# Masks added by VectorE: the attention maxima and the windowed exponentials of a five-layer kernel

## The chip, the cores and the metric
The kernel runs on one core of a Trainium2 chip. The metric is the device time of one execution in microseconds; the time before is the median of three runs.

## The reference
16 sequences of 256 tokens and 256 features go through five attention layers of 16 heads (16 features each), with float32 inputs and outputs: `self` and `cross` (each with an integer mask over query and key, then layer norm, then, behind `cross`, a feed-forward part), `l1` (no mask), `l2` (one key and value head for all, and a window: a query sees the keys from 64 before to 64 after it) and `l3` (no mask, then a second feed-forward part). What the change touches is the masked softmax:

```python
energy = jnp.where(mask == 0, jnp.float32(-1e+20), energy)          # self, cross
attn = jax.nn.softmax(energy / jnp.sqrt(jnp.float32(E)), axis=-1)
...
keep = _window_mask(S)                                              # l2
scores = jnp.where(keep[None, None], scores, NEG)
probs = jax.nn.softmax(scores, axis=-1)
attn = jnp.matmul(probs, v)
```

## The kernel before
A sequence is worked as a list of steps, and each layer's attention goes through its heads twice. In the steps `max0` to `max7` (two heads each, a *unit*) TensorE computes the scores with queries on the partitions into a bank of PSUM (`scores_for_max`, L1290 the mask, L1294 the scores) and VectorE takes minus the maximum over the keys (L1144) into `neg_max`. GpSimd cuts four units' maxima into three bfloat16 pieces (`pieces0`, `pieces1`, L844 to L850), TensorE turns them (`turn0`, `turn1`, L1434), ScalarE copies them out (L934), and a DMA puts them under the queries as three more rows. In the steps `exp0` to `exp7` TensorE computes the scores again, now with keys on the partitions and with the maximum subtracted by those rows (`scores_for_exp`; masks L1314 and L1318, scores L1321 and L1326), and ScalarE takes the exponential into one of four buffers of `probs` (L927). `weigh0` to `weigh3` multiply them with the values (L1347 to L1358); each waits for the exponentials of its two units. Every unit has two halves, t or k = 0 and 1, each in one bank of 2 x 256 float32; for `l2` only the 192 keys or queries in reach are computed, so a bank holds 2 x 192.

The masks are bfloat16 tiles of 0 and -2^66: `neg_self` and `neg_cross`, made by GpSimd (L785), and the constant `neg_band` for `l2`. A mask reaches a bank in one of two ways. Either TensorE multiplies it by an identity with start=True and lets the scores accumulate on it, or the unit is *primed*: ScalarE copies the mask into the bank ahead of the scores (steps `pre0` and so on for maxima, `prx0` and so on for exponentials, L912) and TensorE adds the scores to it. `PRIMED` has for each masked step and each of the 16 sequences eight bits, one for each unit, that say which are primed.

The order of all steps of all sequences is one list, `SCHEDULE`, written out as the string `ORDER`: each character names a lane (0 to f are the sequences' main chains, A to P the work beside them, s the setup, Q to l the priming steps), and takes the next step of that lane. Three or so sequences are in work at a time. Every engine and the DMA queue walk the same list in order and do their own part of each step, with semaphores between them; `place_banks` deals the eight PSUM banks out by the same list.

Of the kernel before, what the change touches and what calls it, by code (L numbers as in the profile page):

```python
# [8 lines left out]
ALU = mybir.AluOpType  # L9
# [14 lines left out]
MASKED = -float(2 ** 66)  # L24
LAYERS = ["self", "cross", "l1", "l2", "l3"]
# [42 lines left out]
for _name in BIAS_SOURCES:  # L68
# [15 lines left out]

PRIMED = {
    ("self", "max"): (
        "00010000 00010010 00001110 01100111 00000001 00000111 00010111 00001111 "
        "01111111 00000001 00000000 00000000 00000000 00010111 01001011 00000100"),
    ("cross", "max"): (
        "11100000 10011111 00000000 11011110 01000100 10000000 11011111 00110001 "  # L90
        "00101000 11110111 00111110 00011100 11100000 00000000 10110101 01001001"),
    ("l2", "max"): (
        "00110000 01000001 10001110 10111111 00110000 10111101 00101101 01101101 "
        "00101000 01000000 00000010 11001100 00011101 10001100 01001100 00000110"),
    ("l2", "exp"): (
        "00000000 10000000 00000000 00000000 00000000 10010000 00000000 00000000 "
        "10100000 00000000 10100000 00000000 10010000 00000000 10100000 00100100"),
# [43 lines left out]
def beside_steps():  # L141
# [8 lines left out]
    "AQ0sA0ss0S0A0Q0AA000QA0BA00001ABsAs0B0A00QA0Q0sAA00R0B101Q0110Q1110BsA11000s00BsRBA01R11R0R1A0RA1001"  # L150
    "0021B1101011AA0CR0s11s1C0020222BBs10001B1121QCQ0Q100BB0s01B1s0CQ0C00001120Q12202100S101S0022012s22SB"
    "02CB0S010Q01QD2BQS2010ss0012S211B10A200RB22R0011s210122AR22R210R1012R20R101211CR01200AAs122sA111102C"
    "0CC0100C12C011111212011001112C0C011110121C00210021010CC20102C20001010002002102B101C2B2000210B202211B"
    "CB201222121022S212122S21221C2121E1122221C1Q02Q120111C200110120S0C11S1221121SQ1010Q120011S002R20012s1"
    "0012R11Q101220100RR200212S00R100120002R10201RQ102R00A21201S11102RR121A0Q1QA20112011112B12A0101E20212"
    "22A10112202022B020221Q2222120Q00R12000012022100200D210200022220122000B1SS0B00B1S02S22S02S0212D01SS20"
    "0222211021201220D02222122S212111102D21Q2021021101D2032S13311231333112301T33232DT13132113T3TC2TC1D2U1"
    "CU331T3T1CC3131331D222333S321333D21333D3E11DDE222U13322D1E3321221331E22432D402F4U2344424EUD144224DDD"
    "2F244242E1234EVE2432QE4UF2224U34E44E2433443V444E2344TE42FE43422443T42ET4T344F23T3423T4323F4RU3E344T4"
    "UTFE2UF3G4SF24F3FF345423U5443F3344U533343U44334345435353335444345343543355VV5553VD5D34534534V45U54V3"  # L160
    "4D4434F44435F5345DUD433555554534433555F35354435552343533F544335343F3G545533335435F45V534333335E45354"
    "5V453355V54E4E5E35353555V443E5F3544555344454555V54544545544534545344454334455TT433544F534F3334TT4435"
    "V4T435UF4T53433TV5454T3433V53U44343T353F5544D3435TUU3344344D5D3453D434D43533544U4W444E4E44354U4555E5"
    "44344554EH44U5554G534445UE545U353454453444545545435355G534435455344543533444435345434344344354444333"
    "534343434V433U433345533335V43X33V443334T55WU3354553VV45VV33534453V54V7VG3355335666GH55V65646655G566W"
    "XG6G5555555556H65G55FGG66W7X77W56G65776675HW6H7W6F67675F35676677565X66FH676657HF5HHHHG677X6H5X7X67G7"
    "7656T6H77557577H6775757575H5H4757775777755IH5765756753755U6756H757XX65HG57V5X56777GX7X7XGG755755755H"
    "5X6777766567775W6777W75576IW56HW5I6566HW5IW6H57H76X685WW8776766I7776688668877668Y66667866768Y7667786"
    "788Y7786Y8767886YI6677668877766YY67I688778777686876878857G86887G8878687867G7J7G7668G7678I8I676788777"
    "678I6766767III7I686I686786776I6J87III68Y866Y886H7Y766678Y6668868878Y666788X8668787867878H688878X886X"  # L170
    "87X87788Y88X8777886YHXH77678I686X8668W7H877Z8I778888Y6IWWI68W6W78777777877X867786W77IWK66877W6668688"
    "76X678876687Z66666W68688W6J86667J6688786786887866788777788G86G788G68X8867G78786G77876876878687677776"
    "866X7766768677766767766786Y787Y87686877Y8676667Y6667688866YY66786766Y78W68Y7h6Y6868878Z68KYg8766a668"
    "99Z989gg897988988899898Z8888JI8Z8gJWI9X98I9898gIYh98I98Jh68J88JK9J9Z8989JhJ89898998g9Jaaaa99K9J8g896"
    "98a89889hh9888a99aJ88K9a999aJ888888L9aa8Kaaa898J8978a89aJ8K8La89aZh98J8K9a98K99aaZ8aaaK89aZKKaZaL89a"
    "K989a89Ka8L9Z9Z8L89bbbaaZ8bbZL9bb9aaaK8aKJbb9b9a99Ka99bbabLba99aKK999gabbJ99b999b99bJLg9bab9Jb999Jba"
    "9gabaaa9L99L9baagaa9gb9Lbbgababb9bga9baga9bbbLabY9abb9b9a99abLLa9aaLbLaaa9LaL9Mbaaa99a9aa9ba9abhL999"
    "bL9ba9ahb9baMh9L99a9ab99aL9bhbhbba9ah9abZbabbLbaab9L9a9bKaa9bbb9aKbKaabbKbbbbb9Kabiabb9bb9aba9aabb9a"
    "ba9999Zb9Zbaabbab99baaagag9bha9hba9a9aba9aZaaibZ9baaa999ab99aab9aZb9bgaZ99b999g9ba9JbbgbK9babb999abb"
    "99iMabZ9bJbJba9baa9b9bbaZagJbbaNagi9bab9bb9aaZbJNag9baiK9abaabbbK9Kg9LgaKb9a9abL9aab9a99Laaab9a99aLa"  # L180
    "a999aabhbbbabL9a99a9bh9bhZhahbbbagh9ahibbab999M99999bbb999baabab9b9abbbba9baabab999ibbbaabbMb9aja9aa"
    "hb9a99cabachcbhacacacMcbMNabcMccMa9bacaMacbaaccbaaaac9MccabcababaccMcbaaccMbcbaccMbbabbcccbNbabccbca"
    "cbaccccbMcbcMbacbbiMbcaNNiacaccZMaONcMcbaciicccdcbcbNbcbiacNbbcNbcNbbbccicicbicbNcdddcOcddbOcdNjccbc"
    "MccbdcbcbccddcdbObcjcbbdecdecejeedOeeceebcejdceMcdcejddcjdNMgkkcdhddedcdkedkcMecdOddcckddMddeeNkddcd"
    "OddeceddckecdecceNddcNOeeecdecNeecNeeccPdecOOOeeccdOOcbcedceddecedecOcPcceceOdddcddcOccedcdOcdeddccc"
    "ddedcdecdOdehejeOecdkddddddeckidecedkekkeeddedckcekikMdecceecejddejdjdMeecccjedeMdciiidMddcieMceceic"
    "ddecceeiedjidcNdeNccicjeNeidcNcjecedcdcPNcecceccdddccecdecceddcdedcddcceePeedcddcccdedecdedecOccOcdd"
    "dddcedOdelccdcedcceddcOcdOededccdcceeccdcececdeecccccecedeececcedceedlccdededciekeeeccjejedcdjeejeed"
    "eceejcecddePjcdcPedkflddffeddejkffecddeeedddeddedPdlkdddefddfffkldeedfdkkeeNNNNedejedekkdkfefdeeePef"
    "leeedjfeNffdededeeffPfdeedfdflPPPffPPdeffdfPeffPfffdkfddfdffdfPfdeffdPPdcefdjdffdeddfededfddflfddOle"  # L190
    "edflfdlfdeddfefffOddlldlfefflfffeefOPffOfdOffPefeffdfffefeffefffefdeeffPjfPfedefefdffdfdefeffeeeefdd"
    "PdffdfffdffffkefeefeeffdeeffffeefefefllPffPffPffffelllffefffefPfefefefPeffeelfefffllfffffffefffefllf"
    "ffffflelffffffffffffffjffffffffffffffffffffffffffffffffffffffffffffffffff"
# [75 lines left out]
FIRST_MASKED = {}  # L269
for _key in SCHEDULE:  # L270
    if _key[2][:3] == "max" and primer(_key) is None:
        FIRST_MASKED.setdefault(_key[:2], _key)
PRIME_NO = Numbers(lambda l, step: step[:3] in ("pre", "prx"))
MAX_NO = Numbers(lambda l, step: step[:3] == "max")
EXP_NO = Numbers(lambda l, step: step[:3] == "exp")
WEIGH_NO = Numbers(lambda l, step: step.startswith("weigh"))
# [92 lines left out]
def width(l):  # L369
    return BAND if l == "l2" else S  # L370


def build(nc, x, ctx, x_features, ctx_features, mask_cross, mask_self, params, setup_params, out):
    stack = ExitStack()
    with stack:
# [98 lines left out]
        exped = sem("exped")  # L474
        weighed = sem("weighed")
# [503 lines left out]
        def _(dve):  # L979
# [148 lines left out]
            def run(keys):  # L1128
                for key in keys:
# [5 lines left out]
                    elif step[:3] == "max":  # L1135
                        u = int(step[3:])
                        n = HALF_NO.place[b, l, f"max{u // 4 * 4}"]
                        if u % 4 == 0 and n >= HALVES:

                            last = HALF_NO.earlier(key, HALVES)  # L1140
                            dve.wait_ge(max_cut, PIECES_NO.upto(last[:2] + (f"pieces{int(last[2][3:]) // 4}",)))
                        for t in range(T):
                            bank = wait_full_unit(dve, key, t)
                            v.tensor_reduce(neg_max[:, n % HALVES, t, 2 * (u % 4):2 * (u % 4) + 2], bank[:, :, 0:width(l)],  # L1144
                                            AX.X, ALU.max, negate=True).then_inc(maxed, 1)
                    elif step in ("ksplit", "qsplit"):
# [504 lines left out]
```

## Time and profile before

| | |
|---|---|
| median of 3 runs | 2375.08 us (2370.65 to 2376.75) |
| profiled execution | 2372.76 us |
| its span, first to last instruction | 2370.6 us |
| granted TensorE clock, mean | 0.984 |
| TensorE matmul busy | 2256.6 us, 95% |
| VectorE busy | 1599.6 us, 67% |
| ScalarE busy | 1297.4 us, 55% |
| GpSimd busy | 517.9 us, 22% |

Busy time is the union of an engine's instructions; instructions of one engine overlap at their ends, so that the time from one start to the next is shorter than the time of one. A row names the line of the kernel, the engine, the operation, what it writes and reads, and how often it ran.

### The profile page before, as it was taken

What the parts mean: (1) busy time and instruction counts of PE and PEld (TensorE: products, weight loads), DVE (VectorE), ACT (ScalarE), POOL (GpSimd) and SP (SyncE); (2) the same over time, 40 slices, a digit from 0 to 9 for tenths busy, and PEclk for the clock granted to TensorE, in tenths of its full rate; (3) what the DMA queues carried; (4) which work ended last, traced back from release to release, by engine and by line L of the source; (5) the groups of instructions that cost most, each with busy time, mean ns of one, the idle gap of its engine ahead of it and who ended that gap; (6) DMA issues with size and microseconds to landing.
All of it is one profiled execution on the core that took longest, in us unless ns stands there. A gap on an engine that the chain in (4) does not pass through costs nothing.

```text
span 2370.6 us, 50134 instructions
## 1 busy us (share of the span) xinstructions
PE 2256.6 (95%) x18291; PEld 1715.8 (72%) x18291; DVE 1599.6 (67%) x3311; ACT 1297.4 (55%) x2723; POOL 517.9 (22%) x1120
## 2 busy tenths in 40 slices
PE   6999999999998999999999999999999999999966
PEld 4777777777776776877767677877778677777744
DVE  6767687775767677576675767676856767586432
ACT  3554556665464656656464656456465654654522
POOL 4221112231112232121212312111232211122100
PEclk9999999999999999999999999999999999999987
DMA  7322213321212133222122332122231321122100
GB/s 224 114 74 60 60 51 86 105 72 35 77 42 69 33 97 82 63 56 71 40 55 71 100 81 58 48 56 72 67 87 51 83 64 42 51 61 53 48 12 12
DMA packets 164242, 159.17 MB, mean 67 GB/s; under 512 B 17824, under 2 KB 162720, under 8 KB 162976
## 3 DMA queue, kind: packets, MB, share of 16 engines
q1 hardware_dynamic: 164000, 155.97, 24.0%
q8 instruction: 148, 2.42, 0.4%
q14 instruction: 94, 0.77, 0.1%
HBM read 35.71 MB, written 4.19 MB: 17 GB/s over the span
## 4 chain that ended last, share of the span: by engine, by line
PE 68%; issue 18%; DVE 5%; POOL 4%; POOLq 3%; ACT 2%; DVEq 1%; DMA 1%; SPq 0%; ACTq 0%
PE bank L1265 16%; PE bank L1255 12%; PE bank L1294 8%; PE bank L1347 7%; PE bank L1326 6%; PE bank L1290 3%; PE bank L1318 3%; PE bank L1246 3%; PE bank L1466 2%; DVE neg_max L1144 2%; PE bank L1321 1%; PE bank L1314 1%; POOL resid L781 1%; POOL rstd L771 1%; PE bank L1496 1%
## 5 line engine op out<-in xcount | busy, mean ns | idle before, releaser
L1144 DVE TENSOR_REDUCE neg_max<-bank 128x2 f32<-128x512 f32 (+1 forms) x1280 | 762.5, 655 | 217.6 <-PE bank L1294 210.7
L927 ACT ACTIVATE probs<-bank 128x512 f32<-128x512 f32 (+1 forms) x1280 | 645.9, 585 | 325.2 <-PE bank L1326 273.4
L1265 PE MATMUL bank<-par,hidden_t 128*128 128x256 f32 x1792 | 418.9, 384 | 6.3 <-ACT hidden_t L862 3.4
L1265 PEld LDWEIGHTS bank<-par,hidden_t 128*128 128x128 f32 x1792 | 334.1, 191 | 58.8 <-ACT hidden_t L862 9.3
L1326 PE MATMUL bank<-query_stack,key_stack 99*128 99x256 bf16 x2048 | 344.4, 274 | 7.2 <-DMA query_stack<-max_rows 4.0
L1294 PE MATMUL bank<-key_stack,query_stack 96*128 96x256 bf16 x2048 | 326.8, 276 | 16.2 <-issue 13.7
L1255 PE MATMUL bank<-tok_t,par 128*128 128x256 f32 x1408 | 334.6, 387 | 4.4 <-ACT tok_t L862 4.4
L1255 PEld LDWEIGHTS bank<-tok_t,par 128*128 128x128 f32 x1408 | 262.2, 193 | 42.6 <-ACT tok_t L862 7.1
L1294 PEld LDWEIGHTS bank<-key_stack,query_stack 96*128 96x128 bf16 x2048 | 195.9, 99 | 111.1 <-issue 33.4
L1347 PE MATMUL bank<-probs,values 128*17 128x256 f32 x4096 | 256.9, 382 | 1.8 <-DVE neg_max L1144 0.9
L1326 PEld LDWEIGHTS bank<-query_stack,key_stack 99*128 99x128 bf16 x2048 | 194.1, 98 | 62.1 <-issue 12.7
L844 POOL CAST max_pieces<-neg_max 128x16 bf16<-128x16 f32 x160 | 37.2, 232 | 821.8 <-DVE neg_max L1144 797.1
L1347 PEld LDWEIGHTS bank<-probs,values 128*17 128x17 f32 x4096 | 102.0, 97 | 109.4 <-issue 29.5
L961 ACT ACTIVATE hidden_t<-bank,par 128x256 f32<-128x256 f32 x256 | 107.0, 472 | 115.5 <-PE bank L1255 114.8
L1029 DVE TENSOR_TENSOR summed<-bank,resid 128x512 f32<-128x512 f32 x64 | 44.1, 690 | 121.3 <-PE bank L1265 121.3
L769 POOL TENSOR_SCALAR var_eps<-mv 128x2 f32<-128x2 f32 x112 | 25.6, 229 | 426.6 <-DVE mv L1000 423.8
L1164 DVE TENSOR_TENSOR hidden_t<-bank,recip 128x256 f32<-128x256 f32 x160 | 99.7, 623 | 12.3 <-issue 0.4
L934 ACT CAST max_rows<-bank 24x256 bf16<-24x256 f32 x160 | 57.0, 356 | 92.1 <-PE bank L1434 91.9
L1318 PE MATMUL bank<-ident_b,neg_self 128*128 128x256 bf16 x512 | 98.3, 273 | 0.0
L1318 PE MATMUL bank<-ident_b,neg_cross 128*128 128x256 bf16 x512 | 97.9, 272 | 0.1
L862 ACT COPY tok_t<-bank 128x512 f32<-128x512 f32 x96 | 56.5, 589 | 72.1 <-PE bank L1246 71.4
L771 POOL TENSOR_TENSOR rstd<-var_eps,minus_half 128x2 f32<-128x2 f32 x128 | 91.6, 716 | 19.4 <-issue 0.9
(167 smaller groups left out, 3271.9 us busy)
## 6 DMA issues: line engine op xcount, KB each, us to landing
query_stack<-query_pieces SPq DMA_DIRECT2D x480, 128.0 KB, 2.4
key_stack<-key_pieces SPq DMA_DIRECT2D x384, 128.0 KB, 2.4
c_in<-in_ctx SPq DMA_DIRECT2D x16, 256.0 KB, 3.3
tok_t<-in_x_features SPq DMA_DIRECT2D x16, 256.0 KB, 2.8
m_in<-in_mask_self SPq DMA_DIRECT2D x16, 256.0 KB, 3.1
x_in<-in_x SPq DMA_DIRECT2D x16, 256.0 KB, 3.1
ctx_t<-in_ctx_features SPq DMA_DIRECT2D x16, 256.0 KB, 3.1
m_in<-in_mask_cross SPq DMA_DIRECT2D x16, 256.0 KB, 3.4
```

Source lines behind the costliest of these rows:

```text
L771: g.tensor_tensor(rstd[:, n % MOMENTS], var_eps[:, n % ROOTS], minus_half[:], ALU.pow).then_inc(rstd_ready, 1)
L927: a_.activation(probs[:, n % PROB_BUFS, k, :, 0:width(l)], bank[:, :, 0:width(l)], ACT.Exp, scale=SCALE[l]).then_inc(exped, 1)
L961: last = a_.activation(hidden_buffer(b, l)[:, f, :], bank[:, k, :], func, bias=pv(bias)[:, f:f + 1])
L1144: v.tensor_reduce(neg_max[:, n % HALVES, t, 2 * (u % 4):2 * (u % 4) + 2], bank[:, :, 0:width(l)], AX.X, ALU.max, negate=True).then_inc(max ...
L1164: v.tensor_tensor(out_tok(b, l)[:, t, :].rearrange("p (c d h) -> p h c d", c=C, h=HC), slots[:, :, 0:HD].rearrange("p (h c) d -> p h c d", ...
L1246: last = pe.transpose(bank[:, c, t * P:(t + 1) * P], src[:, t, c * P:(c + 1) * P], ident[:])
L1255: last = pe.matmul(bank[:, k, :], pv(weight, C)[:, c, column + k * P:column + (k + 1) * P], src[:, c, :], start=(k == 0 and c == 0), stop= ...
L1265: last = pe.matmul(bank[:, t, :], src[:, t * P:(t + 1) * P], weight, start=(t == 0 and n == 0), stop=(n == len(parts) - 1), skip_group_che ...
L1294: last = pe.matmul(bank[:, i, 0:n], queries[0:ROWS, h, t * P:(t + 1) * P], keys[0:ROWS, 0 if l == "l2" else h, columns(l, t)], start=l not ...
L1318: pe.matmul(bank[:, :, t * P:(t + 1) * P], masked[:, t, k * P:(k + 1) * P], twice(ident_b[:], P), start=(t == 0), stop=False, skip_group_c ...
L1326: last = pe.matmul(bank[:, i, 0:n], keys[0:MAX_ROWS, h, k * P:(k + 1) * P], queries[0:MAX_ROWS, h, columns(l, k)], start=l not in neg and ...
L1347: last = pe.matmul(dst, values[b % SLOTS][:, k, head_in(NJ * g + j), :], p, start=(k == 0 and g % 2 == 0), stop=(k == T - 1), skip_group_c ...
```

## The change
Two more ways for the mask, chosen unit by unit by two new tables. A unit whose bit is set in `PRIMED` stays primed.

- A unit with its bit in `ADDED` (maxima of `self`, `cross` and `l2`): TensorE computes the bare scores, and VectorE does, for each of the two heads of a bank, one `tensor_tensor_reduce` that adds the mask in place, multiplies by -1 and takes the minimum, instead of one `tensor_reduce` for both heads.
- A unit with its bit in `CAPPED` (exponentials of `l2`): TensorE computes the scores with the maximum subtracted and without mask, ScalarE takes the exponential, and VectorE takes the elementwise minimum with (mask + 2^66), which is 0 out of reach and 2^66 within it. The weighing waits for VectorE's semaphore `caps` for such units.

`PRIMED` and `ORDER` are other ones, and the lane of priming steps has a `self.pre0` more and `l2.prx0 l2.prx1` in place of `l2.prx0 l2.prx2 l2.prx3 l2.prx5`. The 41 lines of `ORDER` are left out here.

```diff
+LARGEST = 3.0e38
...
+ADDED = {
+    ("self", "max"): (
+        "00000000 00000000 01100000 00111000 11000000 11111011 10000000 00001000 "
+        "11111001 00100000 10100000 10110000 00001001 11100100 01100000 00100100"),
+    ("cross", "max"): (
+        "00000000 01010111 00000010 01101010 00001000 00000000 01011011 00000000 "
+        "00000000 01110111 10100000 01111001 00000011 00101000 00000010 00000000"),
+    ("l2", "max"): (
+        "11001111 00000000 00000000 10010010 00000001 01101101 00001000 10000010 "
+        "00101010 01100010 00000000 10110000 11011000 01111010 10010000 00000111"),
+}
+CAPPED = (
+    "00000101 00000000 10000001 10000001 10100000 00100000 10100000 10100000 "
+    "01111001 11100001 10100000 00100000 00111001 11100000 00000000 10101001"
+)
 PRIMED = {
     ("self", "max"): (
-        "00010000 00010010 00001110 01100111 00000001 00000111 00010111 00001111 "
-        "01111111 00000001 00000000 00000000 00000000 00010111 01001011 00000100"),
+        "11100010 00001001 00000111 00000001 00000100 00000100 00001110 00010111 "
+        "00000110 00000100 00000000 00000000 00000000 00010011 00011100 00000010"),
     ("cross", "max"): (
-        "11100000 10011111 00000000 11011110 01000100 10000000 11011111 00110001 "
-        "00101000 11110111 00111110 00011100 11100000 00000000 10110101 01001001"),
+        "11111000 10101000 00000000 10010100 11110000 11000000 10100100 10000101 "
+        "11001100 10001000 01010110 00000000 01111000 00000000 11111101 00011110"),
     ("l2", "max"): (
-        "00110000 01000001 10001110 10111111 00110000 10111101 00101101 01101101 "
-        "00101000 01000000 00000010 11001100 00011101 10001100 01001100 00000110"),
+        "00100000 01001001 01011110 01101101 11100000 00010010 01110000 00110100 "
+        "10010001 10000000 00000000 00000100 00100101 00000101 01100000 01011000"),
     ("l2", "exp"): (
-        "00000000 10000000 00000000 00000000 00000000 10010000 00000000 00000000 "
-        "10100000 00000000 10100000 00000000 10010000 00000000 10100000 00100100"),
+        "00000000 00000000 00000000 00000000 00000000 11000000 00000000 00000000 "
+        "10000000 00000000 00000000 10000000 10000000 00000000 00000000 00000000"),
 }
...
+def added(key):
+    b, l, step = key
+    row = ADDED.get((l, step[:3]))
+    return row is not None and row.split()[b][int(step[3:])] == "1" and not primes(b, l, step)
+
+def capped(key):
+    b, l, step = key
+    return l == "l2" and step[:3] == "exp" and CAPPED.split()[b][int(step[3:])] == "1" and not primes(b, l, step)
...
+                        if key == FIRST_ADDED.get((b, l)):
+                            if l != "l2":
+                                dve.wait_ge(negs, NEG_NO.upto((b, "self", "inputs" if l == "self" else "negc")))
+                            elif b < SLOTS:
+                                dve.wait_ge(band_ready, 1)
                         for t in range(T):
                             bank = wait_full_unit(dve, key, t)
+                            if added(key):
+                                k = width(l)
+                                for i in range(2):
+                                    h = 2 * (u % 4) + i
+                                    last = v.tensor_tensor_reduce(bank[:, i, 0:k], bank[:, i, 0:k],
+                                                                  neg[l][s][:, t, 0:k], -1.0, LARGEST, ALU.add,
+                                                                  ALU.min, neg_max[:, n % HALVES, t, h:h + 1])
+                                last.then_inc(maxed, 1)
+                                continue
...
+                    elif step[:3] == "exp":
+                        if capped(key):
+                            p = probs[:, EXP_NO.place[key] % PROB_BUFS]
...
+                            for k in range(T):
+                                dve.wait_ge(exped, T * EXP_NO.place[key] + k + 1)
+                                v.scalar_tensor_tensor(out=p[:, k, :, 0:n], in0=twice(neg["l2"][s][:, k, 0:n], n),
+                                                       scalar=-MASKED, in1=p[:, k, :, 0:n], op0=ALU.add,
+                                                       op1=ALU.min).then_inc(caps, 1)
...
-                masked = neg[l][b % SLOTS] if l in neg and primer(key) is None else None
+                fresh = l not in neg or added(key)
+                masked = neg[l][b % SLOTS] if not fresh and primer(key) is None else None
...
-                                         start=l not in neg and i == 0, stop=i == 1, skip_group_check=True)
+                                         start=fresh and i == 0, stop=i == 1, skip_group_check=True)
...
-                masked = neg[l][b % SLOTS] if l in neg and primer(key) is None else None
+                fresh = l not in neg or capped(key)
+                masked = neg[l][b % SLOTS] if not fresh and primer(key) is None else None
...
-                    pe.wait_ge(exped, max(T * EXP_NO.place[b, l, f"exp{2 * g + i}"] + k + 1 for i in range(2)))
+                    exps = [(b, l, f"exp{2 * g + i}") for i in range(2)]
+                    for places, ready in ((EXP_NO.place, exped), (CAP_NO.place, caps)):
+                        left = [T * places[x] + k + 1 for x in exps if (ready is caps) == capped(x)]
+                        if left:
+                            pe.wait_ge(ready, max(left))
```

## Rows read from the trace of the kernel before
**Rows 1.** The page: the span, and each engine's busy us, share and instructions.
```profile
span 2370.6 us, 50134 instructions
PE 2256.6 (95%) x18291; PEld 1715.8 (72%) x18291; DVE 1599.6 (67%) x3311; ACT 1297.4 (55%) x2723; POOL 517.9 (22%) x1120
```
**Rows 2.** Windows: stretch and length, busy PE, PEld, DVE, ACT, POOL, clock, DMA, GB/s.
```profile
0.00:60.00 60.00, 41.42 (x279) 24.39 (x280) 41.64 (x79) 22.28 (x36) 27.90 (x43) 1.00 0.72 222
60.00:2100.00 2040.00, 1990.84 (x16397) 1524.54 (x16395) 1425.40 (x2960) 1162.14 (x2453) 453.14 (x990) 0.99 0.25 67
2100.00:2300.00 200.00, 178.61 (x1389) 135.29 (x1386) 115.51 (x240) 96.12 (x200) 32.27 (x75) 0.97 0.15 42
2300.00:2371.00 71.00, 45.67 (x232) 31.55 (x232) 17.07 (x34) 16.91 (x34) 4.57 (x13) 0.73 0.06 16
```
**Rows 3.** Windows of the tile neg_band alone: busy PE, PEld, ACT, POOL.
```profile
2100.00:2300.00 200.00, 7.88 (x24) 2.32 (x24) 3.57 (x8) 0.00 (x0) 0.97 0.15 42
```
**Rows 4.** Waits of PE: who waited for whom, us in total, times, longest.
```profile
PE bank L1246 <- DVE norm L1008: 11.8, 5, 3.7
PE bank L1434 <- POOL max_pieces L850: 9.1, 10, 2.5
```
**Rows 5.** Lines by form, PE: count, busy us, mean ns, idle before.
```profile
L1314 PE MATMUL bank<-neg_band,ident_b 128*128 128x384 bf16 x230 | 75.1, 327 | 0.4 <-DMA query_stack<-max_rows 0.2 <-ACT probs L927 0.2
L1290 PE MATMUL bank<-neg_self,ident_b 128*128 128x512 bf16 x176 | 68.3, 388 | 11.3 <-issue 11.1 <-DVE neg_max L1144 0.2
```
**Rows 6.** Timeline of PE: start, us, instruction, count; cross masks and scores.
```profile
1081.12 0.38 PE L1290 MATMUL bank<-neg_cross,ident_b 128*128 128x512 bf16 x1
1081.34 0.38 PE L1294 MATMUL bank<-key_stack,query_stack 96*128 96x256 bf16 x2
```
**Rows 7.** Timeline of PE: local masks, with a local score behind each.
```profile
1142.71 0.33 PE L1314 MATMUL bank<-neg_band,ident_b 128*128 128x384 bf16 x1
...
1144.03 0.33 PE L1314 MATMUL bank<-neg_band,ident_b 128*128 128x384 bf16 x1
```
**Rows 8.** Lines by form, ACT: the priming copies.
```profile
L912 ACT CAST bank<-neg_cross 128x512 f32<-128x512 bf16 x112 | 62.1, 600 | 3.2 <-DVE neg_max L1144 3.0
L912 ACT CAST bank<-neg_band 128x384 f32<-128x384 bf16 x130 | 58.4, 495 | 5.6 <-DVE neg_max L1144 4.9 <-DVE key_rest L1058 0.5
```
**Rows 9.** Timeline of DVE: tensor_tensor_reduce on SBUF, with its accumulator read.
```profile
317.82 0.43 DVE L1216 CUSTOM_DVE_ANT_0 hidden_t<-norm 128x256 f32<-128x256 f32 x1
318.17 0.08 DVE L1216 DVE_READ_ACCUMULATOR2_ANT sumsq<- 128x1 f32 x1
318.17 0.42 DVE L1216 CUSTOM_DVE_ANT_0 hidden_t<-norm 128x256 f32<-128x256 f32 x1
```
**Rows 10.** Timeline of DVE, and its group by form: the wide maxima.
```profile
1080.08 4.88 DVE L1144 TENSOR_REDUCE neg_max<-bank 128x2 f32<-128x512 f32 x8 [3.53 <-PE bank L1294]
L1144 DVE TENSOR_REDUCE neg_max<-bank 128x2 f32<-128x512 f32 x1024 | 636.9, 682 | 155.6 <-PE bank L1294 151.0 <-POOL max_pieces L850 1.4
```
**Rows 11.** Timeline of DVE: local maxima, and one alone.
```profile
1148.15 1.48 DVE L1144 TENSOR_REDUCE neg_max<-bank 128x2 f32<-128x384 f32 x3
L1144 DVE TENSOR_REDUCE neg_max<-bank 128x2 f32<-128x384 f32 x256 | 125.6, 549 | 61.9 <-PE bank L1294 59.7 <-POOL max_pieces L850 1.3
```
**Rows 12.** Lines by form, DVE: two-input operations by width and source.
```profile
L1029 DVE TENSOR_TENSOR summed<-bank,resid 128x512 f32<-128x512 f32 x64 | 44.1, 690 | 121.3 <-PE bank L1265 121.3
L1024 DVE SCALAR_TENSOR_TENSOR resid<-hidden_t,rstd,par 128x256 f32<-128x256 f32 x96 | 42.5, 483 | 5.7 <-POOL rstd L771 5.6
L1208 DVE SCALAR_TENSOR_TENSOR hidden_t<-hidden_t 128x512 f32<-128x512 f32 x16 | 11.0, 687 | 5.0 <-ACT hidden_t L966 4.8
```
**Rows 13.** The page's groups: GpSimd's cast of maxima.
```profile
L844 POOL CAST max_pieces<-neg_max 128x16 bf16<-128x16 f32 x160 | 37.2, 232 | 821.8 <-DVE neg_max L1144 797.1
```
**Rows 14.** Timelines of POOL and DVE at 1069 us.
```profile
1069.17 0.58 POOL L844 CAST max_pieces<-neg_max 128x16 bf16<-128x16 f32 x1 [3.22 <-DVE neg_max L1144]
1069.02 0.68 DVE L1041 TENSOR_TENSOR key_rest<-ctx_t,key_pieces 128x512 f32<-128x512 f32 x1
```

More of the change, by code:

```diff
@@ L129 @@
 PRIMES = (
-    "self.pre2 self.pre1 self.pre3 self.pre4 self.pre6 self.pre5 self.pre7 cross.pre0 cross.pre2 cross.pre1 "
-    "cross.pre3 cross.pre4 cross.pre5 cross.pre7 cross.pre6 l2.pre0 l2.pre1 l2.pre2 l2.pre3 l2.pre4 l2.pre5 "
-    "l2.pre7 l2.pre6 l2.prx0 l2.prx2 l2.prx3 l2.prx5 "
+    "self.pre0 self.pre2 self.pre1 self.pre3 self.pre4 self.pre6 self.pre5 self.pre7 cross.pre0 cross.pre2 "
+    "cross.pre1 cross.pre3 cross.pre4 cross.pre5 cross.pre7 cross.pre6 l2.pre0 l2.pre1 l2.pre2 l2.pre3 l2.pre4 "
+    "l2.pre5 l2.pre7 l2.pre6 l2.prx0 l2.prx1 "
 )
@@ L155 @@
[L155 to L164, printed above, removed]
@@ L190 @@
[L190 to L193, printed above, removed]
+    "s00sAAARsAA00000Q00QQS0QAAAAsB01AA0QA0BBQ0As0BQ0A0000101100Q101R0B1B01BA0001R0s0A00ss011AR11001A0S0R"
@@ new lines @@
+    "sRCR10C1B1R10110s1121A00221s20112B00s10Cs01BB111SQQ00BSsQ0Q01S001Q110Q20s01B0002B120C0220100B1C0B012"
+    "0BQB2C200112200B01SQs020102S21S0211s202A20100R2212212AA2R2010RTR2s1R1R1A000RA1C011DR2102011020021C12"
+    "11C101C102C012112C11Cs0C211010011s1001211102012001210C100C02122C20C21C01211000B002000120210210B1202B"
+    "BB01200C2210221T2S0212S1221S012SC22122Q1S2C111R21122211221Q1000S201011C12S111S0221Q02011100021102120"
+    "1C201211Q0Q0211022QRR010000021RRQ0R2102E1010022000Q010RERT121012AV21011A01220s1201111A20B11122101012"
@@ new lines @@
+    "0A2121R10A2122202102B2TR020212202222001000221202120B002S001T20020200000SS2210121B02T2002D2S0SS21Q202"
+    "021002S2S1022B12120Q220202222VS12221D0111222100D2121011112T01323331D233DU33332112D011311331223111E1U"
+    "CT3231C1CCD3C123U1U133322223313331D233033312D312232132D31D2S23V31D1D33213224ED3422434E244243D4421224"
+    "F22DEE42D24U344E4DEE2EU224U444F34T43F22E4T422343E4U1E42ET4F4E24424433E4234F4T44EF3234T4323T2334344T3"
+    "33324TF243F4EU544F42U4F3344UF3U3434F53334344535343V3354554434353355D34VV35553335U534VD53U45V55U34444"
@@ L194 @@
+    "flffOfdlOflelddfflfeffeffdfkefdOffffffeefffffOfdfeeeffffkfedPeefedfffPfeeedfdfefePfdfddfdfPfffdeffee"
+    "ffefeefeffeffefeefeffefefPfffffffdeeffflfeffefefefefflfPefefPfleflfPfflefflfflfffefffeffffPffffflfff"
+    "fffffffffffflffffflffffffffffffffffffffffffffffffffffffff"
 )
@@ L268 @@
 WORK_NO = Numbers(lambda l, step: step in THROUGH_WORK)
-FIRST_MASKED = {}
+FIRST_MASKED, FIRST_ADDED = {}, {}
 for _key in SCHEDULE:
     if _key[2][:3] == "max" and primer(_key) is None:
-        FIRST_MASKED.setdefault(_key[:2], _key)
+        (FIRST_ADDED if added(_key) else FIRST_MASKED).setdefault(_key[:2], _key)
 PRIME_NO = Numbers(lambda l, step: step[:3] in ("pre", "prx"))
@@ L275 @@
 EXP_NO = Numbers(lambda l, step: step[:3] == "exp")
+CAP_NO = Numbers(lambda l, step: step[:3] == "exp", lambda key: capped(key))
 WEIGH_NO = Numbers(lambda l, step: step.startswith("weigh"))
@@ L474, in build @@
         exped = sem("exped")
+        caps = sem("caps")
         weighed = sem("weighed")
@@ L1322, in scores_for_exp @@
                                          queries[0:MAX_ROWS, 2 * u:2 * u + 2, columns(l, k)],
-                                         start=False, stop=True, skip_group_check=True)
+                                         start=fresh, stop=True, skip_group_check=True)
                     for i in range(2 if l != "l2" else 0):
```

63 lines of the change are left out of this document (33 added, 30 removed).

## The prediction
> **What bounds the kernel now.** I read the page's busy shares first. TensorE works 2256.6 us of a span of 2370.6 us, 95%, VectorE 67% and ScalarE 55% [rows 1]. Then the windows, which say where the missing 5% lies [rows 2]: between 60 and 2100 us TensorE is busy 1990.8 of 2040 us, so only 49 us are open there, while the start (18.6 open of 60), the last stretch of two sequences (21.4 of 200) and the end (25 of 71) hold the other 65. The reader is to see that for 86% of the time TensorE is the bound with hardly a hole, VectorE has 30% of that stretch free (1425 of 2040) and ScalarE 43%. What TensorE gives up in that stretch therefore comes off the end time nearly one for one, and what VectorE takes on costs only where it makes TensorE wait. Such waits are small today: the longest sort is 11.8 us over all, that on GpSimd's cut maxima 9.1 us [rows 4].
>
> **Count of the change.** A unit is two heads of one attention step, done in two halves of one PSUM bank each. A unit's mask reaches the bank in one of these ways: by a TensorE matmul (masked), by a ScalarE copy ahead of the scores (primed), and now also by VectorE (added, capped). Counting the 0/1 rows of the diff, with a primed bit taking precedence, gives: self maxima 88 masked and 40 primed become 61, 29 and 38 added; cross 72 and 56 become 46, 48 and 34; local (l2) 76 and 52 become 47, 40 and 41; local exponentials 115 and 13 become 87, 5 and 36 capped. The counts before agree with the trace, two matmuls a unit: 176 for self maxima, 230 for local exponentials [rows 5], and likewise 144 and 152.
>
> **TensorE, removed.** 27 + 26 = 53 self and cross units lose two mask matmuls of 512 columns, 29 + 28 = 57 local units two of 384. The mean of one (388, 327 ns) includes the tail that runs under the next; what it costs the queue is the distance to the next start. For 512 columns that is 1081.34 - 1081.12 = 0.22 us [rows 6]. For 384 columns, from 1142.71 to 1144.03 run four pairs of mask and score matmul of equal width, 1.32 / 8 = 0.165 us [rows 7]. Sum: 106 x 0.22 + 114 x 0.165 = 23.3 + 18.8 = 42.1 us. No other matmul is added or taken away. The score matmuls now open the bank themselves, which is a flag and costs nothing (bounds: that of a first-in-bank matmul like the mask's, after which [rows 6] shows no gap, so 0). Few masks lie where TensorE has holes: of 382 local ones 24 come after 2100 us [rows 3], and beside them the first units of the first sequence. I take 2 us off: 40.
>
> **ScalarE, removed.** Primed units fall by 11 + 8 wide and 12 + 8 narrow, two copies each: 38 x 0.60 + 40 x 0.495 = 42.6 us [rows 8]. ScalarE is on the critical path only in small pieces, so I book nothing; it makes room beside the exponentials, and banks are held shorter, since a primed bank is taken before its scores and an added one is not.
>
> **VectorE, added in the maxima.** An added half is two instructions that add the mask, take the minimum of the negated sum and hand over an accumulator, in place of one reduction. The trace shows this instruction only on SBUF, 256 wide: starts at 317.82 and 318.17, and the accumulator read falls in between, so 0.35 us each [rows 9]. The reduction it replaces: eight 512-wide ones in 4.88 us, the last 0.68 long, so (4.88 - 0.68) / 7 = 0.60 us [rows 10]; three 384-wide ones in 1.48, so (1.48 - 0.55) / 2 = 0.465 [rows 11]. Their difference, 0.135 us for 128 elements, puts the 192-wide new instruction at 0.35 - 0.067 = 0.283. Per wide unit 4 x 0.35 - 2 x 0.60 = +0.20 us, x 72 = 14.4; per local unit 4 x 0.283 - 2 x 0.465 = +0.20, x 41 = 8.3. Sum 22.7 us. Bounds: low 0, if from PSUM it starts no later than a reduction of the same number of elements; high, if nothing overlaps, 4 x (0.43 + 0.08) - 1.20 = +0.84 a unit, 95 us. I take 22.7, for PSUM is no slower where the trace has both: 512 elements with one operand from PSUM 690 ns, 512 from SBUF alone 687 ns [rows 12].
> The Trainium skill ("VectorE: DVE Perf Modes", the errata section) gives a PSUM source a fixed part of 120 cycles against 58; by that 452 instructions would cost 62 cycles or 0.065 us more each, an estimate of 29 us more of VectorE. By that rule the sum for VectorE would be 52 instead of 23 us; [rows 12] don't show the difference.
>
> **VectorE, added in the exponentials.** 36 units x 2 instructions of 384 elements with both tensors in SBUF. 256 elements take 483 ns and 512 take 687 [rows 12], so about 585 ns; as a reduction's last 0.08 us lie under the next (0.68 against 0.60), I take 0.505. 72 x 0.505 = 36 us; bounds 0.40 (the reduction's 0.135 us for 128 elements and nothing fixed) and 0.69 each, 29 to 50 us. Each capping waits for the exponential of ScalarE, and queued behind it on VectorE are the next maxima, whose pieces go to GpSimd, then to TensorE and to the next exponentials; the weighing of a capped unit waits for VectorE instead of ScalarE. Where the order leaves one exponential's length between, the wait is hidden. It has four buffers of probabilities for that, and each is now held about 0.5 us longer.
> VectorE in all: +59 us, so about 1659 us of 2335, 71% against 67%. In the dense stretch it goes from 70% to about 74%. That is not a bound. What is late next is a chance coincidence: a maximum that waits behind a capping. I price it at 4 us of TensorE: the two sorts of wait in [rows 4] sum to 21 us, and busy over free time of VectorE in the dense stretch rises from 0.70 / 0.30 to 0.74 / 0.26, a fifth. Bounds: -15 (a new order removes a third of the 49 open us) and +25 (the open share of the dense stretch grows by half).
>
> **GpSimd.** Its work is the same. The capping has two SBUF inputs; beside such an instruction (1069.02, two SBUF inputs) a piece cast took 0.58 us where the mean is 232 ns [rows 13, 14]. 36 cappings meet few of the 160 chains of pieces; I book nothing, bounds 0 to 3 us.
> The Trainium skill ("SBUF — State Buffer", Who interferes with whom) says that such an instruction shares its second read path with GpSimd and the one that starts later is blocked whole; the trace agrees, and the 452 new mask additions, with one SBUF input, would by it not count.
>
> **Moved.** The whole order is another one, on all queues, SP's loads and copies and GpSimd's steps too. The work and the DMAs are the same in number. After the last step of the last but one sequence comes the same chain, 65 steps and now 68, so I leave the end at its time; at the start a primed first unit makes ScalarE wait for the mask where TensorE did. Bounds for the start: 5 us either way of 18.6 open.
>
> **Sum.** 2370.6 - 40 + 4 = 2334.6 us of span; the profiled run is 2372.8, 2.1 more than its span, and the median of the runs 2375.1, 4.4 more than the span. On the median: 2375.1 - 36 = 2339 us.
>
> **Rivals.**
> 1. The new order also closes holes: the removed copies on ScalarE and shorter-held banks let TensorE run denser. For it: 49 open us in the dense stretch and 65 elsewhere. Against: the order before was as dense, and VectorE has more to do. A third to a half of the 49: 2339 - 4 - 15 to -24, about 2316 us. Chance 0.18.
> 2. The gain is mostly eaten: each 0.5 us capping and its wait stands in VectorE's queue ahead of maxima on the way to the next exponentials. If half of VectorE's added 59 us come back as waits of TensorE, 2375 - 40 + 30 = 2365 us. For it: VectorE is the next busiest. Against: 30% of it is free in the dense stretch. Chance 0.10.
> 3. Slower: the mask addition on PSUM doesn't overlap and reads both operands at half rate, so one takes about 0.69 us (the 512-element price) + 0.08, 4 x 0.77 - 1.20 = +1.9 us a unit, 113 units = 212 us, with the capping 248. VectorE then has 1848 us, 78% of the span, and in places with several added units in a row it sets the pace. It decides from the point where waits take over 40 us; at a quarter, 62 us, the result is 2375 - 40 + 62 = 2397 us. For it: the trace has no such instruction on PSUM. Against: 0.35 us on SBUF, and [rows 12]. Chance 0.06.
> 4. The change does as told, at the forecast's size: 0.66.
>
> **Range and chances.** The forecast with its own bounds (-15 to +25, VectorE's prices inside these) is 2320 to 2360. It must reach towards rival 1 and 2: 2314 to 2364 us. A change under 0.3%, 7 us, is about what can't be told from none. Faster 0.86: forecast, rival 1 and the better part of rival 2 (2365 lies 10 us below). Same 0.06, slower 0.08.
>
> **What would show it.** Mask matmuls of TensorE at 122, 92, 94 and 174, and TensorE's busy time down by 38 to 45 us; no more than 55 us open between 60 us and 270 us before the end. The new instruction pair 0.33 to 0.42 us apart from start to start; above 0.6 the third rival holds. VectorE's busy time up by 50 to 85 us, ScalarE's down by 40. Waits of TensorE on the capped probabilities below 10 us in all. The forecast is wrong if TensorE's busy time falls as said and the span doesn't.

## The result, and the profile after

The changed kernel takes 2338.16 us (median of four runs, 2336.47 to 2344.41) against 2375.41 us; the ratio is 0.9852, 95% interval 0.9829 to 0.9874, so 37 us or 1.5% faster. Measured again with six executions it was 0.9875 (0.9851 to 0.9899), 30 us. The forecast was 2339 us, with 2314 to 2364 as its range. The profiled execution was the slowest of the four, 2344.4 us; its numbers are set against the profiled one of before, 2372.8, and not against the medians. One of the four executions of run 2 below had a granted clock of 0.84 where the others had 0.98 and took 2602.9 us; the figures of run 2 are those of the other three.

The page of the changed kernel, busy us, share and instructions of each engine, for [rows 1]:
```profile
span 2342.3 us, 50407 instructions
PE 2227.5 (95%) x18071; PEld 1699.2 (73%) x18071; DVE 1675.2 (72%) x4061; ACT 1267.8 (54%) x2647; POOL 523.5 (22%) x1120
```
TensorE has 220 matmuls less, as counted. Its window rows, for [rows 2] (the last two stretches are as far from the end as there):
```profile
0.00:60.00 60.00, 43.36 (x252) 25.09 (x253) 38.54 (x74) 23.87 (x39) 27.49 (x41) 0.91 0.76 221
60.00:2072.00 2012.00, 1960.82 (x16180) 1508.88 (x16179) 1496.74 (x3677) 1128.94 (x2373) 457.99 (x991) 0.99 0.25 68
2072.00:2272.00 200.00, 177.27 (x1409) 134.25 (x1407) 122.57 (x275) 97.95 (x203) 32.98 (x76) 0.97 0.15 41
2272.00:2343.00 71.00, 46.01 (x232) 30.95 (x232) 17.36 (x37) 17.00 (x34) 5.00 (x14) 0.74 0.06 16
```
The dense stretch, from 60 us to 271 us before the end, became 28 us shorter (2012 against 2040), and the time in it in which TensorE was open (not busy) stayed: 2012 - 1961 = 51 us against 49. VectorE is busy for 74% of it (1497 of 2012). The end takes what it took. The count of masks left on TensorE, for [rows 5]:
```profile
L1372 PE MATMUL bank<-neg_band,ident_b 128*128 128x384 bf16 x174 | 56.9, 327 | 2.3 <-DMA query_stack<-max_rows 1.3 <-ACT probs L958 1.0
L1347 PE MATMUL bank<-neg_self,ident_b 128*128 128x512 bf16 x122 | 49.7, 407 | 7.7 <-DMA key_stack<-key_pieces 6.8 <-issue 0.7 <-DVE neg_max L1189 0.2
```
The new instruction on VectorE, for [rows 9]; the timeline shows start, us, instruction; first 256 wide, then, in a second stretch, 192 wide:
```profile
978.37 0.43 DVE L1184 CUSTOM_DVE_ANT_0 bank<-bank,neg_self 128x256 f32<-128x256 f32 x1 [0.62 <-PE bank L1351]
978.72 0.14 DVE L1184 DVE_READ_ACCUMULATOR2_ANT neg_max<- 128x1 f32 x1
978.72 0.47 DVE L1184 CUSTOM_DVE_ANT_0 bank<-bank,neg_self 128x256 f32<-128x256 f32 x1
...
979.11 0.47 DVE L1184 CUSTOM_DVE_ANT_0 bank<-bank,neg_self 128x256 f32<-128x256 f32 x1
...
979.49 0.47 DVE L1184 CUSTOM_DVE_ANT_0 bank<-bank,neg_self 128x256 f32<-128x256 f32 x1
```
```profile
272.44 0.40 DVE L1184 CUSTOM_DVE_ANT_0 bank<-bank,neg_band 128x192 f32<-128x192 f32 x1
...
272.75 0.41 DVE L1184 CUSTOM_DVE_ANT_0 bank<-bank,neg_band 128x192 f32<-128x192 f32 x1
...
273.07 0.40 DVE L1184 CUSTOM_DVE_ANT_0 bank<-bank,neg_band 128x192 f32<-128x192 f32 x1
```
Within a row of such instructions starts are 0.38 us apart for 256 (978.72, 979.11, 979.49) and 0.315 for 192; the accumulator read takes 0.14 where it took 0.08 on SBUF. The capping in the timeline, four in 1.96 us, the last 0.55, so (1.96 - 0.55) / 3 = 0.47 us each; and then its group by line, with what it waited for in all:
```profile
1145.26 1.96 DVE L1199 SCALAR_TENSOR_TENSOR probs<-neg_band,probs 128x384 f32<-128x384 bf16 x4
```
```profile
L1199 DVE SCALAR_TENSOR_TENSOR probs<-neg_band,probs 128x384 f32<-128x384 bf16 x72 | 35.8, 550 | 24.2 <-ACT probs L958 24.0
```
VectorE waited 24 us at the cappings, in nine waits, and the matmuls' list of waits has none for a capped exponential (the weight loads' has one, 0.2 us). TensorE's waits in the changed kernel, for [rows 4] (total, times, longest):
```profile
PE bank L1496 <- POOL max_pieces L881: 13.8, 16, 2.2
PE bank L1302 <- DVE norm L1039: 10.9, 8, 3.7
```
The wait for the pieces, which GpSimd cuts from VectorE's maxima, rose by 4.7 us (13.8 against 9.1).

### The profile page after: what moved, and what is told of

Its sections match the earlier page's. It is cut to its first block, busy times and chain, and to the rows that moved or that the text cites. A ratio compares the mean times of both kernels' runs of the same rounds, so it can differ in the third digit from the quotient of the medians.

```text
span 2342.3 us, 50407 instructions
## 1 busy us (share of the span) xinstructions
PE 2227.5 (95%) x18071; PEld 1699.2 (73%) x18071; DVE 1675.2 (72%) x4061; ACT 1267.8 (54%) x2647; POOL 523.5 (22%) x1120
## 4 chain that ended last, share of the span: by engine, by line
PE 63%; issue 19%; DVE 6%; POOL 4%; POOLq 2%; DMA 2%; ACT 2%; DVEq 1%; SPq 1%; ACTq 0%
PE bank L1321 14%; PE bank L1311 11%; PE bank L1409 8%; PE bank L1351 8%; PE bank L1384 7%; PE bank L1376 3%; PE bank L1302 3%; DVE neg_max L1189 2%; PE bank L1528 2%; PE bank L1347 2%; SPq L706 1%; POOL rstd L802 1%; POOL resid L812 1%; PE bank L1558 1%; PE bank L1379 1%
## 5 line engine op out<-in xcount | busy, mean ns | idle before, releaser
L1189 DVE TENSOR_REDUCE neg_max<-bank 128x2 f32<-128x512 f32 (+1 forms) x1054 | 634.0, 658 | 107.8 <-PE bank L1351 102.3
L1351 PE MATMUL bank<-key_stack,query_stack 96*128 96x256 bf16 x2048 | 318.1, 279 | 20.7 <-issue 11.3
L1528 PE MATMUL bank<-ident,hidden_t 128*128 128x128 f32 x640 | 91.2, 276 | 5.8 <-ACT hidden_t L972 4.3
```

The costliest lines, as they stand in the source:

```text
L1351: last = pe.matmul(bank[:, i, 0:n], queries[0:ROWS, h, t * P:(t + 1) * P], keys[0:ROWS, 0 if l == "l2" else h, columns(l, t)], start=fresh ...
L1528: last = pe.transpose(flatten(bank[:])[:, g * P:(g + 1) * P], out_t(b, l)[:, g, t * P:(t + 1) * P], ident[:])
```

## The experiments

All times are medians. The runs were taken in three sets, 1 to 4, 5 to 8 and 9 to 12, beside which the kernel before stood at 2371.9, 2369.3 and 2369.5 us; every run has its ratio to that. Runs 1 to 4 are compared with the changed kernel's 2338.2, which is from a set of its own (before: 2375.4). By ratios a difference may come out some 5 us otherwise, as 0.9852 and 0.9875 for the same kernel show. "Masks" is the change of TensorE's mask time against the changed kernel, by the two prices of the prediction, 0.22 us for 512 columns and 0.165 for 384. A, B, C and so on are the theories named in the text ahead of each run.

**1. All masks back on TensorE, the new order kept.**
```diff
 def added(key): ...
-    return row is not None and row.split()[b][int(step[3:])] == "1" and not primes(b, l, step)
+    return False
 def capped(key): ...
-    return l == "l2" and step[:3] == "exp" and CAPPED.split()[b][int(step[3:])] == "1" and not primes(b, l, step)
+    return False
```


> The new order and the new primed units, but no unit is added or capped: their 113 + 36 masks go back to TensorE, 144 matmuls of 512 columns and 154 of 384, and VectorE loses about 70 us of work. Theory A (the gain is TensorE's mask time, and VectorE's new work costs about nothing): 144 x 0.22 + 154 x 0.165 = 57 us more than the changed kernel, 2395 us, slower than the kernel before. Rival B (the gain is that of the new order and of fewer copies on ScalarE): about as fast as the changed kernel, 2338 to 2350. Rival C (half of VectorE's work comes back as waits of TensorE): 57 - 35 = 22 us more, 2360.


Measured 2391.9 us, ratio 1.0085 (1.0061 to 1.0109): 54 us slower than the changed kernel for 57 us of masks. (By ratios it is 50 to 55 us.) Theory A holds, B falls: without the masks' move the new order brings nothing. Against the kernel before this one is 20 us slower, and 15 of these are masks again, for it has 39 primed units fewer (148 us of masks against 133, by the same prices). The other 5 us are not accounted for by masks.

**2. Added, not capped** (only the second line of that edit).


> New order, maxima added as in the changed kernel, no exponentials capped: 72 mask matmuls of 384 columns go back to TensorE (+11.9 us), VectorE loses 72 cappings (-34 us) and the weighing waits for ScalarE again. A: 2338 + 12 = 2350. B: 2338. C: 2338 + 12 - 17 = 2333, faster than the changed kernel.


Measured 2343.8 us, ratio 0.9895 (0.9864 to 0.9925): +6 us by medians and +10 by ratios (0.9895 against 0.9852), for +12. The interval is 7 us either way: A's 2350 (ratio 0.9908) lies in it, C's 2333 (0.9836) outside, and B's 2338 (0.9857) only just outside. A, but this run alone would not decide it.

**3. Capped, not added** (only the first).


> New order, exponentials capped, no maxima added: 144 mask matmuls of 512 and 82 of 384 columns go back to TensorE (+45 us), VectorE loses 113 x 0.33 = 37 us. A: 2338 + 45 = 2383. B: 2338. C: 2338 + 45 - 18 = 2365.


Measured 2382.5 us, ratio 1.0039 (1.0027 to 1.0050): +44 for +45. A, and the two parts sum to the whole within what can be told: 6 to 10 and 44 against 54. The medians of runs 1 and 3 lie 3 and 1 us from A's numbers and 32 and 18 from C's; for run 2 it is 6 and 11.

**4. All 267 unprimed maxima added.**
```diff
 def added(key): ...
-    return row is not None and row.split()[b][int(step[3:])] == "1" and not primes(b, l, step)
+    return row is not None and not primes(b, l, step)
```


> New order, every maximum that is not primed is added by VectorE (267 units, not 113), the cappings stay: TensorE loses 214 matmuls of 512 and 94 of 384 columns, 62.4 us, VectorE gains 154 x 0.33 = 51 us, some 1725 us in all. The order was not searched for that. A: 2338 - 62 plus a few us, 2280 to 2290. C: 2338 - 62 + 25 = 2301. A third, D (the order was made for VectorE's load as it is, and any more in the dense stretches is waited for in full): 2338 - 62 + 51 = 2327 or more.


Measured 2354.6 us, ratio 0.9935 (0.9917 to 0.9954): 16 us slower than the changed kernel, with 62 us less of masks on TensorE. A, with 2280 to 2290, fails by about 70 us; D said 2327 or more, and it is 28 more. Its dense stretch, its two longest sorts of wait of TensorE behind VectorE's work, and a third that the changed kernel doesn't have, scores put down to a mask addition that ended late:
```profile
60.00:2082.00 2022.00, 1929.95 (x15884) 1473.71 (x15882) 1535.50 (x4502) 1129.52 (x2370) 454.85 (x987) 0.99 0.25 67
```
```profile
PE bank L1496 <- POOL max_pieces L881: 20.3, 21, 3.4
PE bank L1302 <- DVE norm L1039: 13.3, 10, 3.7
PE bank L1351 <- DVE neg_max L1184: 6.7, 14, 1.4
```
TensorE is open for 2022 - 1930 = 92 us, not 51, though VectorE is busy for only 76% of the stretch.

**5. The changed kernel again**, as a control of the next three.


> The changed kernel again, beside the next three on the same chip, for small differences. 2338 us.


Measured 2340.1 us, ratio 0.9875 (0.9851 to 0.9899). Its dense stretch has 48 us open:
```profile
60.00:2067.00 2007.00, 1959.22 (x16195) 1508.57 (x16194) 1498.84 (x3680) 1130.42 (x2375) 459.64 (x994) 0.99 0.25 68
```

**6. 50 more added, where VectorE idles.** The changed kernel has 154 units whose maxima TensorE masks. For each, the idle time of VectorE within 3 us behind it was summed in the trace. The edit sets the bits of the 50 with most.
```diff
 ADDED = {
     ("self", "max"): (
-        "00000000 00000000 01100000 00111000 11000000 11111011 10000000 00001000 "
+        "00000100 11110100 01100000 10111000 11010000 11111011 10000000 00001000 "
...
```


> The changed kernel with 50 more maxima added by VectorE: of the 154 masked ones those behind which VectorE is idle most within 3 us in the trace of the changed kernel (0.72 us in the mean). TensorE loses 20 us of masks, VectorE gains 16 us. Theory D-local (VectorE's work is free where VectorE is idle right behind it, and delays the pieces where it is not): most of the 20 us are kept, about 2338 - 15 = 2323 us, faster than both kernels. Rival (what decides is VectorE's load on the average of the dense stretch, whose price rose from none to all between 72 and 74% busy): the 50 cost a third of what the 154 of the run before did in waits, (17 + 62) / 3 = 26 us, 2338 - 20 + 26 = 2344.


Measured 2338.5 us, ratio 0.9874 (0.9851 to 0.9896): no difference from the control. The 20 us of masks were not kept, so D-local, with 2323, is wrong; its rival's 2344 is ratio 0.9893 and just inside the interval.

**7. 50 more added, where VectorE doesn't idle.** The same edit with the 50 least.


> The same with the 50 behind which VectorE is idle least (0.04 us in the mean); TensorE loses 21 us, VectorE gains 16 us. D-local: their time and what they delay is waited for, 2338 - 21 + 30 or more, 2347 to 2355 us, well above the run with the other 50. Rival (average load): the same 2344 as the other 50.


Measured 2347.9 us, ratio 0.9911 (0.9886 to 0.9935): 8 us slower than the control and 9 slower than its twin, with the same instructions in number. So the place counts, which the theory of the average load denies, though its 2344 alone is inside this interval too. That idle time is what makes the place count isn't shown by it: the two fifties differ in more (local units 16 and 8, first units of the four whose maxima are cut together 4 and 21). In the dense stretch TensorE is open for 58 us in run 6 and 64 in run 7:
```profile
60.00:2063.00 2003.00, 1945.48 (x16109) 1497.66 (x16102) 1509.01 (x3942) 1129.22 (x2370) 457.77 (x989) 0.99 0.25 68
```
```profile
60.00:2078.00 2018.00, 1954.30 (x16110) 1500.99 (x16108) 1511.46 (x3944) 1130.64 (x2375) 459.29 (x994) 0.99 0.25 68
```

**8. VectorE's new work left out.**
```diff
-                                for i in range(2):
-                                    h = 2 * (u % 4) + i
-                                    last = v.tensor_tensor_reduce(...)
+                                last = v.tensor_reduce(neg_max[...], bank[:, :, 0:k], AX.X, ALU.max, negate=True)
...
-                        if capped(key):
+                        if False:
...
```
In the part left out the weighing waits for ScalarE's exponentials alone again.

> The changed kernel without the work that it gave VectorE: the added units take the plain reduction of scores without mask, and the capped ones keep their exponentials out of reach, so that masks are left out in part of the units. TensorE's and ScalarE's instructions are those of the changed kernel. VectorE loses 70 us. Theory A (its new work costs next to nothing in the searched order): 2338 - 4, at most 2338 - 8 = 2330. Rival C (a third to a half comes back): 2303 to 2315.


Measured 2342.6 us, ratio 0.9889 (0.9859 to 0.9919): nothing gained, though VectorE's busy time fell by 67 us (from the control's 1672.8):
```profile
PE 2225.2 (95%) x18071; PEld 1700.0 (73%) x18071; DVE 1605.7 (69%) x3311; ACT 1268.2 (54%) x2647; POOL 522.0 (22%) x1120
```
C, with 2315 or less, falls. A's 4 to 8 us didn't come either. By the two ratios (0.9889 +- 0.0030, 0.9875 +- 0.0024) the work that VectorE took over costs at most some 6 us in the changed kernel; 4 us and nothing can't be told apart.

**9. The old order with the new tables.**
```diff
 PRIMED = ...   # as before the change
 PRIMES = ...   # as before the change
 ORDER = ...    # as before the change
```


> The order and the primed units of the kernel before, with the new tables of added and capped units on top (where a unit isn't primed: 63 added, 31 capped). TensorE loses 35 us of masks against the kernel before, VectorE gains 50 us, ScalarE nothing. A (TensorE's mask time is the gain, wherever VectorE takes it up): 2372 - 35 + 3 = 2340 us. S (the order has to leave VectorE room at just these units): waits eat most of it, 2360 to 2375 us.


Measured 2367.0 us, ratio 0.9988 (0.9976 to 1.0000): 35 us of masks less than before, and 3 us gained. S's time holds; its reason, that waits for VectorE eat the gain, is not shown, since no run left the masks out in the old order. In the profile TensorE is open for 64 us of the dense stretch, 15 more than before:
```profile
60.00:2089.00 2029.00, 1965.33 (x16181) 1500.34 (x16183) 1469.03 (x3383) 1160.71 (x2450) 454.47 (x988) 0.99 0.25 67
```

**10. The 154 without any mask.** As run 4, but the 154 that run 4 adds beyond the changed kernel take the plain reduction of bare scores (`ALSO_ADDED` is the changed kernel's `ADDED`).
```diff
-                            if added(key):
+                            if added(key) and ALSO_ADDED[(l, "max")].split()[b][u] == "1":
```


> As the run in which all 267 maxima not primed are added, but the 154 units that the changed kernel masks on TensorE get no mask at all: bare scores and the plain reduction, so that these masks are left out. TensorE's instructions are those of that run (62 us less than the changed kernel), VectorE's work is that of the changed kernel. V (that run stood at 2355 instead of 2276 since VectorE took longer for its maxima): 2338 - 62 plus a few, about 2280 us. Q (TensorE, let go of its masks, runs into something else that the order has at the same place, VectorE's plain reductions and what follows them): 2320 or more.


Measured 2325.1 us, ratio 0.9812 (0.9793 to 0.9832). With VectorE's work as in the changed kernel, 62 us less on TensorE bring 15 us against the control (0.9812 against 0.9875), or 10 against the first ratio, 0.9852. Q holds: most of the gain was not there to be had in this order. Its dense stretch has 70 us open, and TensorE waits longer for the pieces than in the changed kernel:
```profile
60.00:2049.00 1989.00, 1918.80 (x15887) 1475.94 (x15886) 1491.01 (x3671) 1125.80 (x2366) 455.65 (x984) 0.99 0.25 69
```
```profile
PE bank L1507 <- POOL max_pieces L892: 17.3, 19, 3.1
```

**11. The idle 50 without mask.**


> As the run with the 50 units behind which VectorE idles, but these 50 get the plain reduction and no mask (left out). TensorE 20 us less than in the changed kernel, VectorE the same. V: 2339 - 20 = 2319 us. Q: 2335 to 2340, as with the masks added by VectorE (2338.5).


Measured 2330.4 us, ratio 0.9830 (0.9807 to 0.9853): about half of the 20 us is kept, 10 us; between V and Q.

**12. The busy 50 without mask.**


> As the run with the 50 units behind which VectorE doesn't idle, but these 50 get the plain reduction and no mask (left out). TensorE 21 us less than in the changed kernel, VectorE the same. V: the 8 us lost and the 21 us expected come back, 2318 us. Q: only the 8 us come back, 2335 to 2340.


Measured 2333.3 us, ratio 0.9848 (0.9830 to 0.9867): a third of the 21 us is kept, 7 us; between V and Q, nearer to Q.

Pairs of these runs have the same instructions on TensorE and differ only in what VectorE does for some units. They give what VectorE's extra time costs:

| units | VectorE's extra | with mask by VectorE | without mask | price, by medians |
|---|---|---|---|---|
| of the changed kernel | 70 us | 2340.1 | 2342.6 | none |
| 50 with idle behind | 16 us | 2338.5 | 2330.4 | 8 us |
| 50 without idle behind | 16 us | 2347.9 | 2333.3 | 15 us |
| all 154 | 51 us | 2354.6 | 2325.1 | 29 us |

The last three rows compare runs of two sets, by ratios 0.44%, 0.63% and 1.23%, that is 10, 15 and 29 us. The intervals of the single ratios are about 0.25% either way, so that the prices of the two fifties differ isn't shown. What is shown, in one set, is that run 7 takes 9 us more than run 6; of this 3 us are there without the masks too (runs 11 and 12). Idle time behind a unit doesn't make it free: the fifty with most of it, 0.72 us in the mean, still cost 8 to 10 us for 16 of VectorE. Of the kernels that compute the whole reference none beats the changed one; run 6 is level with it.

## Why the prediction was right

**TensorE's masks (term of -40 us): right, and shown in this order.** Runs 1, 2 and 3 return 54, 6 to 10 and 44 us for 57, 12 and 45. The reason it gave, that what TensorE gives up in the dense stretch comes off nearly one for one, is too general. It held for the masks that went with the new order. In the old order the same sort of edit kept 3 of 35 us (run 9), and in the new order the next 62 us brought 10 to 15 even where VectorE was asked nothing more (run 10). A share of 95% with 49 us open doesn't say that a second limit is far: of the next 20 us only a third to a half came off (runs 11 and 12). Runs 4 and 10 show more waiting for the pieces of the maxima (20.3 and 17.3 us against 13.8), so part of it may be the path from bare scores over VectorE's reduction and GpSimd's cut back to TensorE. These 3.5 us are small beside the 47 that run 10 lacks, and what the rest is stays open; the order of banks and copies is one candidate that no run tried.

**VectorE's work (sized 59 us, priced 4): the price within what can be told, the size 11 us short.** With the measured distances the sum is 72 x (4 x 0.38 - 1.20) + 41 x (4 x 0.315 - 0.93) + 72 x 0.47 = 23 + 14 + 34 = 70 us; busy time, which counts ends that overlap, rose by 75.6. The mis-sized term is the mask addition, 0.33 us a unit and not 0.20, since it starts every 0.38 us on PSUM where [rows 9] had 0.35 on SBUF. [Rows 12], from which no difference was concluded, compare instructions that need not behave alike here. It didn't matter: run 8 finds no cost of all of it, within some 6 us. The forecast called a maximum behind a capping a chance coincidence. The places of the added units don't look like chance: in the changed kernel's trace the median idle time of VectorE within 3 us behind an added unit is 0.46 us, behind a masked one 0.18, and more of the second kind had a price (the table's last three rows).
The Trainium skill ("VectorE: DVE Perf Modes", the errata section) gives a PSUM source 62 cycles more than SBUF, 0.065 us. The trace has 0.03 us more from start to start, half of it (the one on SBUF reads one float32 tensor, this one the bank and a bfloat16 mask), and 0.06 us more in the accumulator read, which lies under the next start.

**ScalarE and GpSimd (nothing): right.** ScalarE's busy time fell by 29.6 us and not by 42.6. The primed copies' lines went from 164.8 us (62.1, 58.4 and 44.3) to 125.6 us (53.0, 40.3 and 32.3), 39.2 us; what is missing to 29.6 is 2.6 us of two more table loads and, for the rest, ends that lay under the next instruction and that busy time never counted. GpSimd's first cast takes 235 ns in the mean against 232, so the cappings did not slow it.

**The order (rival 1, a gain beyond the masks; nothing booked at the start): no gain, and a cost at the start that was not foreseen.** Open time did not fall. What did change is the clock of the start: 0.91 and 0.74 over the first 60 us in the two profiles of the changed kernel, 0.91 with all masks back (run 1), and 1.00 in both profiles of the old order (before and run 9). It goes with the order, not with VectorE's work. The second profile of the changed kernel and then the kernel before, 0 to 90 us in thirds, the granted clock third from the end:
```profile
0.00:30.00 30.00, 18.78 (x67) 9.90 (x68) 19.14 (x43) 11.74 (x15) 18.67 (x27) 0.75 0.87 253
30.00:60.00 30.00, 23.62 (x169) 14.11 (x168) 14.28 (x28) 11.15 (x22) 7.32 (x11) 0.74 0.69 190
60.00:90.00 30.00, 27.78 (x206) 22.28 (x208) 22.54 (x56) 9.83 (x20) 5.18 (x13) 0.83 0.44 130
```
```profile
0.00:30.00 30.00, 13.91 (x50) 7.35 (x51) 16.57 (x31) 7.22 (x7) 16.11 (x24) 1.00 0.86 264
30.00:60.00 30.00, 27.51 (x230) 17.05 (x230) 25.07 (x48) 15.06 (x30) 11.79 (x20) 1.00 0.58 181
60.00:90.00 30.00, 27.78 (x210) 22.07 (x208) 21.81 (x53) 13.09 (x25) 5.00 (x8) 0.89 0.45 138
```
By these rows TensorE stood at the lower level, 1.2 instead of 2.4 GHz, for 30 x 2 x (0.25 + 0.26 + 0.17) = 41 us of the 90 instead of 7; in the first 30 us, where it fell, TensorE was busy for 18.8 us instead of 13.9. It has done 442 matmuls where it had done 490; without the masks 371 have started instead of 402. The 31 are 5 to 7 us at 0.165 to 0.22 us each, an estimate, and part of them is another mix of work. That is the size of what is missing between the 42 us of masks removed and the 37 gained, but it was not measured by itself.

**What the trace was to show.** Mask counts and the waits at the cappings came as said. TensorE's busy time was to fall by 38 to 45 us and fell by 29.1 (31.0 in the second profile): that test was badly chosen, as busy time counts the tail of each matmul, so that holes shorter than a tail are in it, and time at half clock too. The span of the two profiles fell by 28.3 and 32.5 us, the medians by 37.

**Rivals 2 and 3** asked for 30 us and 62 us of returned waits; run 8 shows none above some 6. Rival 3 falls with the 0.38 us from start to start too. Waits that VectorE's work brings back do exist outside the change: in run 4 they are 29 us, by the table, behind mask additions and not, as rival 2 had it, behind cappings.

**The time itself** was met within 1 us, which is luck. The same kernel gained 37 us by the first ratio and 30 by the second, the 4 us for VectorE can't be told from nothing, and the cost at the start was not in the sum.

## What to carry to other kernels
A busy share of 95% doesn't promise that work moved off the engine pays in full: here 57 us paid 54 in the order that came with the move, 35 us paid 3 in another, and 62 us more paid 10 to 15. Price a second helping by a run that simply leaves the work out (run 10 here), before looking at the engine that would take it. The receiving engine's mean share says little about the price: the same 50-unit edit at two choices of place was worth 0 or 8 us at the same share, and idle time right behind the moved work is a first guide to the place, not a guarantee. And test an order and its tables apart: here each without the other was worth little or less than nothing (2367 against 2370, and 2392 against 2372, of which 15 are the primed units given up).

## What was not expected of the hardware
- The mask addition with an accumulator starts every 0.38 us for 256 and 0.315 us for 192 elements out of PSUM in place, and 0.35 us for 256 on SBUF, and its accumulator read takes 0.14 us against 0.08. The 64 elements between the two widths cost 0.065 us, so a start every 0.12 us plus about 1 ns an element; the plain reductions out of PSUM, 0.60 us for 512 and 0.465 for 384, come by the same working to 0.06 us plus 1.05 ns.
- Two SBUF inputs, one of them bfloat16, 384 elements: a start every 0.47 us, where the prediction took 0.505.
- The granted clock in the first 60 us was 0.91 and 0.74 in two profiles of the changed kernel, and 1.00 in the two of the old order, with the DMA queues moving 221 to 224 GB/s in all four.
